# Masking the causal triangle in the probabilities instead of in the scores

## The reference

```
scores = einsum('bhtd,bhsd->bhts', q, k) / sqrt(D) + slopes * pos
scores = where(causal, scores, -inf)
y = einsum('bhts,bhsd->bhtd', softmax(scores), v) @ w_proj + b_proj
x = x + y
logits = rms_normalised(layernorm(x) @ gate_w.T + gate_b); g = top1(softmax(logits / 0.5))
h = gelu(einsum('nd,edh->neh', layernorm(x), w1) + b1)
out = x + ((einsum('neh,ehd->ned', h, w2) + b2) * norm_g).sum(1)
```

## Time and profile before

| | before |
|---|---|
| median of 3 runs | 322.9 us (321.93 to 322.92) |
| span of the profiled execution | 321.8 us |
| PE busy | 299.8 us, 93% |
| DVE busy | 190.8 us, 59% |
| ACT busy | 194.0 us, 60% |
| POOL busy | 75.8 us, 24% |
| mask products (L766) | 192, of 128 or 256 columns |

### The profile page before, as it was taken

The page is one execution under the profiler, slowest core; times in us unless marked ns, Lnnn a source line. Parts: engine busy times, 40 slices in busy tenths (PEclk is TensorE's granted clock), DMA queues, the critical chain, the costliest instruction groups (busy, mean ns, idle before and its releaser), DMA issues.

```text
span 321.8 us, 5579 instructions
## 1 busy us (share of the span) xinstructions
PE 299.8 (93%) x1816; PEld 193.3 (60%) x1817; DVE 190.8 (59%) x789; ACT 194.0 (60%) x323; POOL 75.8 (24%) x211
## 2 busy tenths in 40 slices
...
DMA packets 12524, 13.23 MB, mean 41 GB/s; under 512 B 2064, under 2 KB 9104, under 8 KB 12240
## 3 DMA queue, kind: packets, MB, share of 16 engines
...
q10 hardware_dynamic: 96, 0.13, 0.2%
...
## 4 chain that ended last, share of the span: by engine, by line
PE 79%; DVE 12%; DMA 3%; issue 2%; ACT 1%; SPq 1%; DVEq 0%; ACTq 0%
PE ffn_bank L853 17%; PE a_ring L760 12%; PE v_ring L738 11%; PE pv_bank L785 11%; PE a_ring L686 5%; PE a_ring L766 5%; DVE unused L1076 5%; PE a_ring L688 4%; PE a_ring L687 4%; DMA q_stack<-q_lo 1%; PE v_ring L814 1%; DMA q_stack<-m_lo 1%; PE v_ring L747 1%; PE v_ring L798 1%; DMA x_in<-x 1%
## 5 line engine op out<-in xcount | busy, mean ns | idle before, releaser
L1076 DVE CUSTOM_DVE_ANT_0 unused<-v_ring,cst 128x512 bf16<-128x512 f32 (+3 forms) x256 | 112.2, 487 | 53.0 <-PE v_ring L738 48.7
L560 ACT ACTIVATE probs<-a_ring 128x512 f32<-128x512 f32 (+1 forms) x192 | 92.5, 526 | 68.2 <-PE a_ring L766 67.2
L738 PE MATMUL v_ring<-k_stack,q_stack 128*128 128x512 f32 (+3 forms) x256 | 88.9, 419 | 6.5 <-DMA q_stack<-q_lo 4.3
L760 PE MATMUL a_ring<-q_stack,k_stack 128*128 128x512 f32 (+3 forms) x256 | 76.9, 360 | 2.0 <-DMA q_stack<-m_lo 2.0
L853 PE MATMUL ffn_bank<-hidden,w_sb 128*128 128x512 f32 x128 | 66.3, 602 | 1.1 <-ACT ffn_T L586 0.7
L738 PEld LDWEIGHTS v_ring<-k_stack,q_stack 128*128 128x128 f32 x256 | 48.9, 207 | 27.0 <-issue 16.8
L577 ACT ACTIVATE hidden<-a_ring,cols_sb 128x512 f32<-128x512 f32 x64 | 43.4, 688 | 32.5 <-PE a_ring L688 32.1
L760 PEld LDWEIGHTS a_ring<-q_stack,k_stack 128*128 128x128 f32 x256 | 46.8, 197 | 9.5 <-issue 5.6
L766 PE MATMUL a_ring<-score_mask,ident_bf 128*128 128x128 bf16 (+1 forms) x192 | 48.2, 252 | 0.0
L785 PE MATMUL pv_bank<-probs,v_ones 128*32 128x256 f32 (+3 forms) x512 | 42.3, 440 | 0.0
L686 PE MATMUL a_ring<-zT_hi,w_hi 128*128 128x512 f32 x64 | 33.0, 516 | 0.8 <-DVEq L975 0.8
...
## 6 DMA issues: line engine op xcount, KB each, us to landing
...
```

What stands on the lines that cost most here:

```text
L560: act.activation(probs[:, n % 2, q, KIND_AT[kind]:KIND_AT[kind] + cols], a_bank()[:, 0:cols], ACT.Exp).then_inc(e_freed, 1)
L738: last = pe.matmul(dst[:, at:at + P * (n + 1)], q_stack[b % 2][:, s, n * P:(n + 1) * P], k_stack[:, s, q, 0:P * (n + 1)], start=True, stop ...
L760: pe.matmul(dst[:, at:at + P * (TB - j)], k_stack[:, s, q, j * P:(j + 1) * P], q_stack[b % 2][:, s, j * P:T], start=(at == 0), stop=False, ...
L1076: ins = dve.tensor_tensor_reduce(unused[:, (uses[0] - 1) % V_BANKS, at:at + cols], bank_[:, at:at + cols], cst[:, C_MASK + T - cols:C_MASK ...
```

## The change

The mask products and their two operands go. POOL instead clears the masked triangle of `probs` after the exponential: `mask_probs` waits for the four exponentials of a kind and runs one `affine_select` over the four heads' diagonal blocks (128 partitions, 4 x 128 elements) for each key block of the kind, so 4 selects a set and 64 in all; `pv` waits for `probs_masked` instead of `e_freed`. So that the exponential stays finite for the pairs far from the diagonal, spare rows of the two stacks (free until now) put -1e30 on the pairs of the upper half of a key block's keys with the lower half of its own block's queries; the rows come in `consts` by one more DMA of 256 KB, and `q_constants` starts from them instead of from zeros. `z_rstd` moves from POOL to DVE (`root_z`, place 9 of step 0). In step 0 `y_high`, `y_norm` and `attention` stand one place later, `pv_last` moves from place 0 to place 3 (early plan) or 2 (later), and ACT takes the upper half of `pv_bank` after three GELU tiles instead of two. POOL's own order is rewritten around the selects.

```diff
@@ -38,7 +38,7 @@
 QR = P // QUADS
 TERMS = 3
 MASKED = -3.0e38
-MASKED_SCORE = -1.0e30
+CORNER_SCORE = -1.0e30
 EPS_LN = 1e-5
 EPS_F32 = 1.1920929e-07
 EPS_GATE = 1e-6
@@ -53,7 +53,7 @@
 MAX_ROWS = MAX_D * ROW_D + CONST_TERM
 
-C_IDENT, C_MASK, C_KEY, C_QUERY, C_QUAD = 0, 128, 640, 1152, 1156
+C_IDENT, C_MASK, C_KEY, C_QUERY, C_QUAD, C_CORNER = 0, 128, 640, 1152, 1156, 1160
 
@@ -63,16 +63,16 @@
 PLACES = 16
 EARLY_PLAN = {
     "max": (-1, 0, 2, 3, 4, 5, 6, 8, 8, 9, 11, 11), "take_max": (12,),
-    "exp": (4, 4, 5, 6, 8, 8, 9, 11, 11, 13, 14, 14), "pv": (11, 15), "pv_last": (0,),
+    "exp": (4, 4, 5, 6, 8, 8, 9, 11, 11, 13, 14, 14), "pv": (11, 15), "pv_last": (3,),
 }
 LATER_PLAN = {
     "max": (-1, -1, 2, 3, 4, 5, 6, 7, 8, 9, 10, 11), "take_max": (13,),
-    "exp": (4, 5, 6, 7, 8, 9, 10, 10, 12, 13, 14, 15), "pv": (12, 15), "pv_last": (0,),
+    "exp": (4, 5, 6, 7, 8, 9, 10, 10, 12, 13, 14, 15), "pv": (12, 15), "pv_last": (2,),
 }
 
 STAGES = {
-    "y_low": (2, 14, 0), "y_high": (0, 4, 1), "y_norm": (0, 5, 1), "attention": (0, 7, 1),
-    "z_norm": (0, 13, 1), "z": (0, 15, 1), "logits": (2, 4, 1), "route": (2, 13, 1), "gates": (3, 13, 1),
+    "y_low": (2, 14, 0), "y_high": (0, 5, 1), "y_norm": (0, 6, 1), "attention": (0, 8, 1),
+    "z_root": (0, 9, 1), "z_norm": (0, 13, 1), "z": (0, 15, 1), "logits": (2, 4, 1), "route": (2, 13, 1), "gates": (3, 13, 1),
     "ffn": (1, 14, 2), "x_stats": (0, 15, -1), "x_norm": (1, 7, -1), "x": (1, 10, -1), "k": (1, 12, -1),
     "q": (1, 15, -1), "v": (1, 14, -1), "b2": (2, 15, 0),
 }
@@ -395,8 +394,9 @@
                 sp.dma_start(out_view[b], result[:]).then_inc(stored, 16)
 
             load_x(0)
-            sp.dma_start(cst[:, C_KEY:], consts[:, C_KEY:]).then_inc(cst_loaded, 16)
+            sp.dma_start(cst[:, C_KEY:C_CORNER], consts[:, C_KEY:C_CORNER]).then_inc(cst_loaded, 16)
             sp.dma_start(w_attn_sb[:], w_attn).then_inc(wa_loaded, 16)
+            sp.dma_start(cst[:, C_CORNER:], consts[:, C_CORNER:]).then_inc(corner_loaded, 16)
             sp.dma_start(cst[:, C_MASK:C_KEY], consts[:, C_MASK:C_KEY]).then_inc(mask_loaded, 16)
             sp.dma_start(cols_sb[:], columns).then_inc(rows_loaded, 16)
             sp.dma_start(rows_sb[:], rows.to_broadcast([P, rows.shape[1]])).then_inc(rows_loaded, 16)
@@ -477,10 +477,16 @@
                 inverse_sqrt(pool, settle, rstd1[:], mv1[:, :, 1], 1.0, EPS_LN, var[:, 0, :], var[:, 1, :])
                 pool.sem_inc(x_rstd_ready, 1)
 
-            def z_rstd(b):
-                pool.wait_ge(z_stats_ready, b + 1)
-                inverse_sqrt(pool, settle, rstd2[:], mv2[:, :, 1], 1.0, EPS_LN, var[:, 0, :], var[:, 1, :])
-                pool.sem_inc(z_rstd_ready, 1)
+            def mask_probs(n, kind):
+
+                pool.wait_ge(e_freed, UNITS * n + QUADS * (kind + 1))
+                at = KIND_AT[kind]
+                for j in KEY_BLOCKS[kind]:
+                    diagonal = probs[:, n % 2, :, at:at + P]
+                    last = pool.affine_select(out=diagonal, in_=diagonal, compare_op=ALU.is_ge, fill=0.0, base=0,
+                                              pattern=[[0, QUADS], [1, P]], channel_multiplier=-1)
+                    at += P * (TB - j)
+                last.then_inc(probs_masked, 1)
 
             def norm_logits(b):
 
@@ -494,10 +500,6 @@
             pool.wait_ge(zeros_set, 1)
             pool.affine_select(out=ident, in_=zeros[:, 0:P], compare_op=ALU.not_equal, fill=1.0, base=0,
                                pattern=[[1, P]], channel_multiplier=-1).then_inc(ident_set, 1)
-            pool.affine_select(out=ident_bf[:], in_=zeros[:, 0:P], compare_op=ALU.not_equal, fill=1.0, base=0,
-                               pattern=[[1, P]], channel_multiplier=-1).then_inc(mask_ready, 1)
-            pool.affine_select(out=score_mask[:], in_=zeros[:, 0:P], compare_op=ALU.is_ge, fill=MASKED_SCORE, base=0,
-                               pattern=[[1, P]], channel_multiplier=-1).then_inc(mask_ready, 1)
             pool.wait_ge(wa_loaded, 16)
             split(w_attn_sb[:], w_attn_hi[:], w_attn_lo[:], wa_split, 0)
             pool.wait_ge(xn_ready, 1)
@@ -520,24 +522,30 @@
 
             for b in range(B):
                 for s in range(SETS):
-                    if s == 0 and b >= 1:
-                        load_k_low(b, 1)
-                        z_rstd(b - 1)
-                    if s == 1 and b + 1 < B:
-                        x_rstd(b + 1)
-                        split_low(b + 1, 0)
-                        split_low(b + 1, 1)
-                    if s == 2 and b + 1 < B:
-                        load_k_low(b + 1, 0)
-                    if s == 2 and b >= 1:
-                        norm_logits(b - 1)
+                    n = SETS * b + s
                     if b == 0 and s == 0:
                         pool.wait_ge(w1_loaded, 16)
                         split(w1_sb[:], w1_hi[:], w1_lo[:], w1_split, 0)
                         pool.wait_ge(rows_loaded, 32)
                         split(gate_sb, gate_parts[:, 0:E], gate_parts[:, E:2 * E], w1_split, 2)
+                    if n >= 1:
+                        mask_probs(n - 1, 2)
+                    if s == 0 and b >= 1:
+                        load_k_low(b, 1)
+                    if s == 1 and b + 1 < B:
+                        x_rstd(b + 1)
+                    if s == 2 and b + 1 < B:
+                        split_low(b + 1, 1)
+                        load_k_low(b + 1, 0)
+                    if s == 2 and b >= 1:
+                        norm_logits(b - 1)
+                    mask_probs(n, 0)
+                    if s == 1 and b + 1 < B:
+                        split_low(b + 1, 0)
+                    mask_probs(n, 1)
                     if s == 2:
                         residual(b)
+            mask_probs(SETS * B - 1, 2)
             norm_logits(B - 1)
 
@@ -602,7 +610,7 @@
 
             def q_constants(i):
                 for s in range(SETS):
-                    act.activation(q_stack[i][:, s, :], zeros[:], ACT.Identity,
+                    act.activation(q_stack[i][:, s, :], cst[:, C_CORNER:], ACT.Identity,
                                    bias=cst[:, C_QUERY + s:C_QUERY + s + 1]).then_inc(q_const, 1)
 
             def k_constants(half):
@@ -615,6 +623,7 @@
             act.activation(lge[:], zeros[:, 0:TB * E].rearrange("p (n e) -> p n e", n=TB), ACT.Exp)
             act.wait_ge(cst_loaded, 16)
             k_constants(0)
+            act.wait_ge(corner_loaded, 16)
             q_constants(0)
             split_high(0, 0)
             split_high(0, 1)
@@ -631,7 +640,7 @@
                         evacuate_ffn(b - 2)
                     fb, tiles = chunk(b, s)
                     for i, m in enumerate(tiles):
-                        if s == 0 and i == 2:
+                        if s == 0 and i == 3:
                             evacuate_pv(b - 1, 1)
                         gelu_tile(fb, m)
                     if s == 0 and b >= 1 and not tiles:
@@ -750,26 +759,20 @@
             def exp_unit(b, s, k):
                 n = SETS * b + s
                 kind, q = k // QUADS, k % QUADS
-                if n == 0 and k == 0:
-                    pe.wait_ge(mask_ready, 2)
                 if k == 0:
                     pe.wait_ge(m_loaded, 32 * (n + 1))
                 dst = a_bank(e_freed, UNITS * n + k + 1)
                 at = 0
                 for j in KEY_BLOCKS[kind]:
-                    pe.matmul(dst[:, at:at + P * (TB - j)], k_stack[:, s, q, j * P:(j + 1) * P],
-                              q_stack[b % 2][:, s, j * P:T], start=(at == 0), stop=False, skip_group_check=True)
+                    last = pe.matmul(dst[:, at:at + P * (TB - j)], k_stack[:, s, q, j * P:(j + 1) * P],
+                                     q_stack[b % 2][:, s, j * P:T], start=True, stop=True)
                     at += P * (TB - j)
-
-                blocks = len(KEY_BLOCKS[kind])
-                diagonal = dst[:].rearrange("p (a t) -> p a t", t=P)[:, 0::3, :][:, 0:blocks, :]
-                pe.matmul(diagonal, ident_bf[:], score_mask[:].unsqueeze(1).to_broadcast([P, blocks, P]),
-                          start=False, stop=True, skip_group_check=True).then_inc(e_filled, 1)
+                last.then_inc(e_filled, 1)
 
             def pv(b, s, kind):
                 n = SETS * b + s
-                pe.wait_ge(e_freed, UNITS * n + QUADS * (kind + 1))
+                pe.wait_ge(probs_masked, KINDS * n + kind + 1)
                 if kind == 0 and s == 0:
                     pe.wait_ge(v_ready, b + 1)
                     if b == 0:
@@ -1180,6 +1183,8 @@
                         take_yT(of)
                     if stage == "attention":
                         take_attention(of)
+                    if stage == "z_root":
+                        root_z(of)
                     if stage == "z_norm":
                         normalise_z(of)
                     if stage == "z":
@@ -1250,7 +1255,7 @@
     import numpy as np
 
```

(7 more changed lines are left out.)

7 lines of the change are left out of this document (3 added, 4 removed).

## The result

| | before | after |
|---|---|---|
| median | 322.9 us | 332.8 us (332.1 to 334.1, 4 runs) |
| ratio to before | | 1.030, 95% interval 1.0275 to 1.0327 |
| span of the profiled execution | 321.8 us | 332.3 us |
| mean granted clock in it | 0.968 | 0.933 |
| PE busy | 299.8 us | 294.3 us |

The change makes the kernel 9.9 us slower. Forecast were 319.3 us and a range up to 327.5, so the time lies outside it, on the side that had 0.28. The profiled execution of the kernel after is the longest of its four, with the lowest granted clock (0.933; the others had 0.943, 0.948 and 0.953).

A forecast was written before the change was run, and what follows sets the result against it. PE's queue was taken to set the pace. Masks 21.5 us saved, less waits of 4.8, 1.4, 0.7 and 11.0, left 3.6 us: 322.9 to 319.3 us, range 311 to 327.5 us for 8 in 10.

The forecast's parts named there:

- the side that had 0.28: Whole kernel: the chance given to the change making it slower by more than about 1 us.
- rival C: Selects on POOL cost 1.13 us each, as four small ones, lengthening PE's waits: 331 us; chance 0.20.
- Rival A: New PE waits mostly covered; only transpose_max waits, 2 us in three sets, plus 0.7 at the end: 308.1 us; chance 0.17.
- rival D: PE's waits move to where ACT is late, 1 or 2 us of gain go: 321 to 323 us; chance 0.10.
- term one: PE's mask products in all sixteen sets: removing them saves 1.35 us a set, 21.5 us.
- kind 2 has 128 mask columns as kind 0 has, and I give it 0.13: PE's kind-2 mask products: priced at 0.13 us each, like kind 0, four in a set.
- Rival B: Removing the masks gives back only what the chain counts, 16 us instead of 21.5: 324.8 us; chance 0.08.
- Term two: Later pv_last and ACT's third GELU tile: only shift work inside the set, costed at nothing.
- The cover named: Exponential units at places 4 to 8: said to cover the later pv_last and ACT's third GELU tile.
- Term three: Granted clock: full in set 8 at 1.00; the forecast's sum held no cost for a lower clock.
- The closing test: PE's new waits at the named points: if they are there and total over 21 us, the change loses.
- Its other test: Sets 7 and 11: shorter by 1.35 us with no new wait; shorter by 1.0 means Rival B holds.

The follow-up runs named there:

- e_late_places: Kernel before with only the change's new places (pv_last, y_high, y_norm, attention, ACT's evacuation), masks and root as they were: 331.4 us, ratio 1.025.
- e_fill: Kernel after with spare products keeping PE busy where it waited in sets 4, 8 and 12: 327.8 us, ratio 1.014.
- e_nomask: Kernel before without its mask products and nothing in their place, the triangle near the diagonal left unmasked: 309.9 us, ratio 0.960.
- e_nosel: Kernel after without its selects, pv waiting for the exponentials alone, the triangle left unmasked: 324.4 us, ratio 1.004.
- e_rootpool: Kernel after with the inverse root of step 0 back on POOL, between the selects of kinds 0 and 1: 328.2 us, ratio 1.016.

## Why the prediction was wrong

**What held.** The select (0.61 forecast, 0.636 measured); with it rival C, which needed 0.77, is out. The waits were at the forecast instructions: `transpose_max` 2.6 us forecast, 1.8, 2.6 and 2.6 measured; `transpose_y_norm` 0.9 and 0.7; `pv` of kind 0 1.6 and 1.1, 1.1, 0.5; kind 1 in set 1 1.4 and 1.0; the end 0.7 and 0.5; set 4's next step of the same chain, the projection, about 0.5 and 0.47. Forecast were 17.9 us in all, measured are 14.3 new ones. Rival A's cover is not there, and of rival D's waits for ACT none over 0.25 us stands in sets 0 to 14. In set 8 the sum was right term by term, too: statistics 3.3 us after the projection's start (3.4 forecast), the root with its stretch 2.85 (2.7), the max units about 2.1 (2.2). The select's 0.61 was in part luck: the line behind it was drawn through one point each of two different operations. The Trainium skill's rule (SBUF — State Buffer, "Who interferes with whom") agrees with the root's two stretched operations and with the max unit at its usual 0.69 us. But z, a `tensor_scalar` with one tensor from SBUF and two per-partition operands, went from 1.11 to 1.82 us beside a select, so instructions with two input tensors are not the only ones that suffer here; the same section counts `tensor_scalar` too among those that can contend. Of the two rates in the Trainium skill, GPSIMD Engine Reference, "Performance pitfalls for Q7 kernels", the measured 0.636 us fits the unrolled one: by the other the select would have been over 0.87 us, an estimate from that page.

**What failed, term one: the masks, 21.5 us, measured 12.9.** Some 3.6 of the 8.6 too much is the price in a set, 1.12 us instead of 1.35, and nearly all of that is the step "kind 2 has 128 mask columns as kind 0 has, and I give it 0.13": it costs 0.07 (0.27 a set instead of 0.52), and in set 9 three of its four masks stand before `pv` or a transpose, not in a row of 512-column products. The other 5 us is the multiplication by sixteen (16 x 1.12 = 17.9). It took PE as the bound in every set, at one price. Sets 6 and 10 give 0.9 each, sets 8 and 12 0.5 each, set 1 nothing, and set 4 is longer by 1.1. Rival B had the sign, and its 16 us is nearer to 12.9 than 21.5 is, but not the mechanism: it doubted the distances, and these are right within a run of the same products.

**Term two: "the later `pv_last` and ACT's third GELU tile only shift work inside the set; I cost them at nothing".** The places alone cost 8.0 us (e_late_places), of which the forecast had only the waits at `transpose_y_norm` (0.64 us each there) and at set 4's projection. 0.33 us a set is `pv_last` taken out of the run of 24 products; most of the rest is step 0, where the later projection makes z late as well (0.90 us in sets 8 and 12). The cover named, the exponential units, hides a wait and not PE's own time. What ACT's third tile costs was not tried by itself.

**Term three: the clock, not in the sum at all.** 5.2 us (e_fill). The sum priced each wait at its length; a stretch at half the clock follows the long ones.

**The account.** Against the kernel before: masks -12.9 (e_nomask), new waits +14.3, clock +5.2 make +6.6 of the +9.9. Of the 3.3 that remain, 2.0 are `pv_last` in the six sets 5, 7, 9, 11, 13 and 14, at 0.33 each (set 5 takes 17.37 us with all masks off PE, 17.03 in e_nomask); the last 1.3 is not told apart (sets 0 to 2 have new waits of 0.5 to 0.7 us, ahead of max units and of the transposes of x, that are not in the sum). The same by experiments that undo parts: masks -12.9, places +8.0, selects +8.4 (e_nosel), and +6.4 left for the root on DVE and what it sets off, of which e_rootpool gave back 4.6; the clock is contained in these. The two accounts overlap and are not to be added. The closing test, "if the waits total over 21 us, the change loses", failed with all three terms: 14 us of new waits were enough. Its other test, sets 7 and 11 shorter by 1.35, or by 1.0 if rival B holds, does not decide: they are shorter by 1.26, 0.44 of which are the transposes of y, now in the set before, and `pv_last` takes 0.33 away. The masks alone give 1.15 to 1.19 there (against e_late_places, and in e_nomask).

**What stays open.** Why set 4 falls to the half clock for 13.7 us and set 8 for 3.4 us is told by nothing more than the waits before them. e_fill filled sets 4, 8 and 12 together and so does not price one wait. ACT's third tile has no run of its own, and in the two kernels with the new POOL order the stages `route` and `gates` moved with it.
